# Last group of a two-half attention loop: GpSimd's final products after the rotations, three softmax heads scaled by ScalarE, VectorE reordered

## What is computed

```
xn = layernorm(x)
s  = attention(xn)        # 32 query heads, 8 key/value heads, head size 128,
                          # rotary embedding, window of 128 tokens, output projection wo
g  = silu(ffn(xn))        # 512 -> 1376 -> 512, weights unpacked from 4-bit values
out = x + s * g
```

## Times and profile before

| | us |
|---|---|
| three runs: lowest, median, highest | 878.37, 878.67, 880.2 |
| profiled execution: its own time | 877.86 |
| its span, first to last instruction | 876.1 |
| mean granted TensorE clock, share of full speed | 0.998 |

### The profile page before, as it was taken

How to read it: one execution, slowest core, us unless ns; L and a number is a source line. 1 busy time by engine, 2 the same in 40 slices (tenths; PEclk the granted TensorE clock), 3 DMA queues, 4 the chain that set the end, 5 groups by cost and what they waited for, 6 DMA issues and landing times.

```text
span 876.1 us, 13995 instructions
## 1 busy us (share of the span) xinstructions
PE 840.6 (96%) x4252; PEld 701.8 (80%) x4252; DVE 600.6 (69%) x1621; ACT 469.7 (54%) x1133; POOL 390.2 (45%) x303
## 2 busy tenths in 40 slices
PE   3999999999989999999999999999999999999887
PEld 3777888888767888888888888888888888888765
DVE  7953554433569677775968586677858676875895
ACT  2474121132577557574756666485748557574641
POOL 0144121124545436552644464184435436552892
PEclk9999999999999999999999999999999999999999
DMA  6200001002010201200120111012000201200211
GB/s 195 56 18 8 13 24 51 19 1 72 1 41 9 74 1 48 73 1 1 48 72 0 48 36 35 0 48 72 0 27 21 72 0 48 72 0 0 61 62 60
DMA packets 40224, 32.55 MB, mean 37 GB/s; under 512 B 5056, under 2 KB 32384, under 8 KB 40192
## 3 DMA queue, kind: packets, MB, share of 16 engines
q1 hardware_dynamic: 40192, 32.16, 12.5%
HBM read 30.05 MB, written 2.10 MB: 37 GB/s over the span
## 4 chain that ended last, share of the span: by engine, by line
PE 82%; DVE 8%; POOL 3%; issue 3%; ACT 3%; DMA 0%; SPq 0%; ACTq 0%; POOLq 0%; DVEq 0%
PE bank L966 25%; PE bank L968 24%; PE bank L967 24%; PE bank L1106 5%; PE bank L1086 3%; DVE probs L815 2%; POOL acc L338 1%; ACT W2raw L433 1%; POOL swap L321 1%; PE bank L986 1%; PE bank L1076 1%; DVE xl L655 1%; POOL acc L342 0%; POOL q L325 0%; DMA xn<-in_L_attn_x 0%
## 5 line engine op out<-in xcount | busy, mean ns | idle before, releaser
L321 POOL TENSOR_TENSOR swap<-swap,cst 128x512 f32<-128x512 f32 x80 | 103.9, 1298 | 248.8 <-ACT swap L488 247.9
L966 PE MATMUL bank<-xh,wih 128*128 128x512 f32 x384 | 158.5, 413 | 0.2 <-DVE q L783 0.2
L968 PE MATMUL bank<-xh,wil 128*128 128x512 f32 x384 | 151.0, 393 | 0.0
L967 PE MATMUL bank<-xl,wih 128*128 128x512 f32 x384 | 150.3, 391 | 0.0
L815 DVE TENSOR_SCALAR probs<-probs,rinv 128x128 f32<-128x128 f32 (+1 forms) x256 | 129.1, 546 | 4.6
L515 ACT ACTIVATE probs<-probs,nmx 128x128 f32<-128x128 f32 (+1 forms) x256 | 113.5, 445 | 33.8 <-DVE nmx L804 33.4
L523 ACT ACTIVATE ph<-bank 128x512 fp32r<-128x512 f32 x96 | 55.6, 597 | 112.2 <-PE bank L1106 110.9
L966 PE MATMUL bank<-woh,oh 128*128 128x512 f32 x256 | 100.4, 392 | 0.3 <-DVE ol L832 0.3
L968 PE MATMUL bank<-woh,ol 128*128 128x512 f32 x256 | 99.9, 390 | 0.0
L967 PE MATMUL bank<-wol,oh 128*128 128x512 f32 x256 | 99.9, 390 | 0.0
L287 POOL TENSOR_TENSOR hl<-act_h,hh 128x512 fp32r<-128x512 f32 x22 | 29.9, 1361 | 148.2 <-ACT hh L416 148.2
(11 more groups left out here) (102 smaller groups left out, 1828.0 us busy)
## 6 DMA issues: line engine op xcount, KB each, us to landing
raw<-in_L_attn_wq SPq DMA_DIRECT2D x32, 256.0 KB, 2.8
raw<-in_L_attn_wo SPq DMA_DIRECT2D x32, 256.0 KB, 2.9
packed<-in_L_ffn_w SPq DMA_DIRECT2D x20, 128.0 KB, 2.2
xn<-in_L_attn_x SPq DMA_DIRECT2D x8, 256.0 KB, 3.5
raw<-in_L_attn_wk SPq DMA_DIRECT2D x8, 256.0 KB, 3.0
raw<-in_L_attn_wv SPq DMA_DIRECT2D x8, 256.0 KB, 2.7
raw<-in_L_attn_x SPq DMA_DIRECT2D x8, 256.0 KB, 2.7
out<-gate SPq DMA_DIRECT2D x8, 256.0 KB, 2.0
```

Source lines behind the costliest of these rows:

```text
L321: nc.gpsimd.tensor_tensor(v, v, spread(sin.unsqueeze(1), P, 2, SEQ), ALU.mult).then_inc(sin_done, 1)
L966: nc.tensor.matmul(out_, sh, mh, start=(i == 0), stop=False)
L967: nc.tensor.matmul(out_, sh, ml, start=False, stop=False)
L968: m = nc.tensor.matmul(out_, sl, mh, start=False, stop=(i == n - 1))
```

## The change

All three parts are in group 7; nothing before `rest(0)` in step 7a changes on any engine.

1. GpSimd, step 7a: `rest(0)` to `rest(3)` no longer stand behind one rotation each but all behind the last rotation (c = 4).
2. Step 7b, heads 1 to 3 of b = 1: VectorE only inverts the sums (the new `inverse`); the two products of a head are made by ScalarE (the new `weigh`, an activation Copy with the inverse as its scale). Head 0 stays with VectorE.
3. VectorE, step 7b: the three `inverse` stand behind `normalise` of head 0, `finish(0, 2)` and `finish(0, 3)`, all ahead of `p_lo(0, 2)`. On ScalarE `weigh` of head 1 stands ahead of `p_hi(0, 2)`, those of heads 2 and 3 behind it.

```diff
@@ GpSimd, step
                 for c in range(1, 5):
                     sin_part(ng, nbp, c)
-                    if w and last:
-                        rest(c - 1)
+                if w and last:
+                    for t in range(4):
+                        rest(t)
@@ ScalarE
+            def weigh(g, bp, b, h):
+                s = 4 * b + h
+                act.wait_ge(rinv_done, cnt(8, g, bp, s + 1))
+                for i, (c0, c1) in enumerate(((0, P), (P, 3 * P))):
+                    m = nc.scalar.activation(probs[:, s, c0:c1], probs[:, s, c0:c1], ACT.Copy,
+                                             scale=rinv[:, s, i:i + 1])
+                m.then_inc(probs_done, 1)
...
                     exps(g, bp, 1, 3)
+                    weigh(g, bp, 1, 1)
                     p_hi(g, bp, 0, 2)
+                    weigh(g, bp, 1, 2)
+                    weigh(g, bp, 1, 3)
@@ VectorE
-            def normalise(g, bp, b, h):
+            def inverse(g, bp, b, h):
                 s = 4 * b + h
                 dve.wait_ge(exp_done, cnt(8, g, bp, s + 1))
                 nc.vector.reciprocal(rinv[:, s, :], rsum[:, s, :]).then_inc(rinv_done, 1)
+
+            def normalise(g, bp, b, h):
+                s = 4 * b + h
+                inverse(g, bp, b, h)
...
                     normalise(g, bp, 1, 0)
+                    inverse(g, bp, 1, 1)
                     finish(0, 2)
-                    normalise(g, bp, 1, 1)
+                    inverse(g, bp, 1, 2)
                     finish(0, 3)
+                    inverse(g, bp, 1, 3)
                     p_lo(g, bp, 0, 2)
-                    normalise(g, bp, 1, 2)
-                    normalise(g, bp, 1, 3)
```

## The result

| us | before | changed |
|---|---|---|
| six runs of each: lowest, median, highest | 877.99, 878.52, 880.2 | 873.65, 873.92, 874.35 |
| ratio of the times, 95% interval | | 0.9941, 0.993 to 0.9952 |
| profiled execution: its own time, its span | 877.86, 876.1 | 874.13, 872.3 |
| mean granted clock | 0.998 | 0.996 |

The medians differ by 4.6 us (0.52%), the ratio, taken round by round, says 0.59%; 873.5 was forecast. Between the two profiled executions it is 3.7 us.

A forecast was written before the change was run, and what follows sets the result against it. TensorE was taken as the bound nearly everywhere, held up by VectorE's products waiting for GpSimd. 4.65 - 1.40 + 1.71 = 4.96 us gave 872.9 by the profiled execution, 873.7 by the median; forecast 873.5, range 871.1 to 876.8.

The forecast's parts named there:

- Step 7a, forecast 4.65 us: Without `rest(0)` between rotations, step 7a runs like 6a: transposes 2.62 us earlier, 2.03 more up to the first output projection.
- More than the whole 4.65 is not there: Upper bound on the move's gain in step 7a, up to the first output projection: at most 4.65 us.
- The cost behind it: Step 7b, b = 0: VectorE's products beside unpaused GpSimd delay the first transposes to 843.33, a 3.2 us wait; 1.40 given back.
- the rule behind them: A VectorE product waits for the running GpSimd instruction's end; one passes at a border, two where GpSimd itself waits a moment.
- The lock takes every border: Rival, chance 0.16: no two products ever pass together, five pairs take 2.75 us each; gain 1.3 us, time 877.4.
- luckier borders: Rival, chance 0.10: heads 1 and 3 each pass one border earlier, transposes start at 840.7; gain 7.5 us, time 871.1.
- The mis-sized term: the clock: Clock fall after 7b's 3.2 us wait, up to 1.7 us, hidden; as rival "slower", chance 0.05, low some 13 us, 888.
- the 1.85 us wait for `finish(0, 2)`: Step 7b: TensorE reaches `attend` at 847.4 and waits until 849.2; a clock fall was to hide behind this.
- the clock is low after 843: A sign, named in advance, that the prediction is wrong: low granted clock after 7b's first transposes, forecast near 843.3.
- ScalarE is the late one: Rival, chance 0.09: a Copy with a column costs 1.6 us a head, second transposes wait until 853.95; gain 3.3, 875.4.
- The rule against part 2: Skill's advice to multiply on VectorE, not ScalarE: heads 0.55 us each instead of about 0.8, part 2 losing 0.75 us.
- The sum: 4.65 - 1.40 before 7b's first transposes + 1.71 between the two transposes = 4.96 us; 872.9 against the profiled execution.

The follow-up runs named there:

- e3: Changed kernel with each `rest` computing 8 of its 512 columns, the other 504 left as they were; 868.25 us, ratio 0.9877.
- e7: Changed kernel with each GpSimd instruction of `rest` split into two of 256 columns; 869.26 us, ratio 0.9888.
- e8: Changed kernel with unread spare matmuls (13, 8 and 3) filling all three TensorE waits of step 7b; 873.62 us, ratio 0.9938.
- e1: Kernel before with part 1 alone: `rest(0)` to `rest(3)` behind the rotations, all heads still on VectorE; 878.17 us, ratio 0.9987.
- e10: Changed kernel with `p_hi(0, 2)` issued ahead of ScalarE's first `weigh`; 873.04 us, ratio 0.9932.
- e5: Changed kernel with ScalarE also multiplying the four heads of b = 0 of step 7b, seven in all; 869.62 us, ratio 0.9898.
- e6: Changed kernel with all eight heads of 7b on ScalarE, inverses and `weigh` of b = 1's heads 0 and 1 earlier; 868.12 us, ratio 0.9879.
- e2: Changed kernel without part 1: `rest(0)` to `rest(3)` between the rotations as before, parts 2 and 3 kept; 875.26 us, ratio 0.9957.
- e11: e6 with `rest(0)` to `rest(3)` back between the rotations, as before the change; 874.71 us, ratio 0.9949.
- e4: Changed kernel with 13 unread spare matmuls of 512 columns ahead of 7b's first transposes, filling one TensorE wait; 875.48 us, ratio 0.9957.
- e9: e1's kernel (all heads on VectorE, old order) with `rest` computing 8 of its 512 columns; 869.04 us, ratio 0.9889.

## Why the prediction was right, and where it was not

- **Step 7a, forecast 4.65 us.** From the first transposes of 7a to the projection it was 31.93 us and is 27.28: 4.65. Taking the times of 6a for a step whose disturbance is removed was exact here. "More than the whole 4.65 is not there" was not: with the fourth rotation earlier, the scores that wait for `ql` came 5.87 us earlier, counted from the first transposes of 7a (37.18 us before, 31.31 after). The pairs of 7b gave 2.98 of these back.
- **The cost behind it.** Forecast: pairs of 1.8, 2.45, 1.5 and 2.4 us, the transposes at 843.33 after a wait of 3.2. Measured: 2.06, 2.50, 1.56 and 2.38, at 843.59 after 3.29. e3 and e7 show the rule behind them, each from another side. "The lock takes every border" fell with the pair of 1.56, "luckier borders" with those of 2.50 and 2.38.
- **The mis-sized term: the clock.** The prediction named the fall, took it to be as long as the one before, up to 1.7 us, and hid it behind the 1.85 us wait for `finish(0, 2)`. It was twice as long, and "the clock is low after 843", one of the prediction's own signs of being wrong, came true. TensorE reached `attend` at 850.34 instead of 847.4, past the end of that cover (849.2). The projection ahead of it, whose bank `finish(0, 3)` reads, was late too, and VectorE waited 0.81 us for that. `p_lo(0, 2)` then waited 0.30 us more for `ph`, which ScalarE makes from the transposes at 849.99, and stood at 851.25 instead of 850.1, the second transposes at 853.56 instead of 852.25. In distances from the start of 7a, the forecast gained 3.25 us up to the first transposes of 7b and 1.71 between these and the second; measured are 2.89 and 0.66. So 0.36 of the forecast 4.96 were lost in the pairs and 1.05 to the clock. e8, with the clock at 1.00, has the forecast distance between the transposes (8.85 for 8.92), which bears this out in the traces. In e1, where the fall was short, `attend` began at 849.42, inside the cover.
- **ScalarE.** 0.80 and 0.74 us a head for a forecast 0.8, ready ahead of need. In the trace of e10 its place ahead of `p_hi` costs nothing. "ScalarE is the late one" fell.
- **The rule against part 2.** By the instruction alone the Trainium skill (ScalarE: Activation LUTs, Rules for kernel authors) is right: 0.55 us a head on VectorE against 0.74 to 0.80. For this kernel it decides the wrong way. e5 and e6 are faster the more of the products leave VectorE, because a product there waits for GpSimd and one on ScalarE does not.
- **The sum.** By the traces the gain is 3.55 us in D and 3.73 in the profiled executions' own times, for 4.96. By the medians it is 4.6. The profiled execution of before lies 0.7 under its median and that of the changed kernel 0.2 above its own, which makes up the difference. So part of the closeness of 873.5 to 873.92 is luck: against the profiled execution 872.9 was forecast and 874.13 came.
- **What the prediction did not see.** It treated the three parts as terms of a sum. e1, e2 and e11 show that they are not: GpSimd's work, moved away from 7a's products, lands beside 7b's, and the move is worth 1 us or 6 according to who makes these.

What stays open: why the clock's fall after the same wait lasted 3.4 us in e1 and 6.8 in the changed kernel and its repeats. The instructions of TensorE are the same up to 846.7, where it came back in e1. In e1 the fall began at about 843.2 (a granted clock of 0.62 over 843 to 844, 1.00 over 842 to 843), in the others at 842.6 to 842.7. No run varied that alone.

## What to carry to other kernels

Before moving an engine's work out of a tight place, follow it to where it lands and ask what it shares with the work there; here two products per head waited for whole GpSimd instructions, and giving these products to ScalarE, or halving GpSimd's instructions, freed what the move alone did not. An engine that is slower per instruction, but is not held up by its neighbour there, can be the faster place. And read the granted clock beside the busy share: a new wait on TensorE has a price behind it that can outlast the cover that was counted for it.

## What the runs showed of the hardware that was not expected

- A wait of about 3.3 us was followed by a stretch at the 1.2 GHz level of 3.4 us (e1) or 6.8 us (changed, e10, and the repeat), though TensorE worked without a gap from the end of the wait on.
- Smaller waits near each other can do it too: e4 fell after 1.57 and 0.56 us of idle time, e1 a second time after 2.29. Yet 2.2 us idle before 854 in the kernel before had no fall, not even with another 1.61 before 857.21, and neither had 1.95 us before `attend`'s second product in e9.
- A GpSimd product or sum over 256 columns mostly takes 0.73 to 0.80 us (e7), over 512 columns mostly 1.26 to 1.30, over 8 columns mostly 0.20 (e3).
